# A LoRA transformer block in fp32: values made between the base products, and probabilities turned in fp32

## The reference, cut to what matters

```
x (8 batches, 128 tokens, 512)                      all in fp32
x = x + x @ W0[id0[b]].T                            base product, one 512x512 matrix per batch
q, k, v = lora(x; wq, aq, bq), lora(.. k), lora(.. v)   32 query heads, 8 key/value heads, D = 128
    lora(x; w, a, b) = x @ w + (x @ a[id1]) @ b[id1]    rank 16
q, k = rope(q), rope(k)                             out = q * cos + swapped(q) * sin
p = softmax(causal(q @ k.T / sqrt(D)));  o = p @ v
x = x + lora(o; wo, ao, bo)
x = x + LoRA 2 (A, B[id0]);  x = x + linear W3, b3 + LoRA 3[id2]
```

## Time and profile before

| what | us |
|---|---|
| median of 3 runs (839.33 to 841.19) | 840.07 |
| the profiled execution | 838.21 |
| its span, first to last instruction | 836.4 |
| PE busy in the span | 758.6 (91%) |
| DVE busy | 606.9 (73%) |
| ACT busy | 360.9 (43%) |
| POOL busy | 327.9 (39%) |
| mean granted TensorE clock | 0.958 of 2.4 GHz |

### The profile page before, as it was taken

One profiled execution on the slowest core, in us unless ns is written; L12 is line 12 of the kernel. 1 busy time (PEld: TensorE's weight loads), 2 busy tenths in 40 slices (PEclk: granted clock), 3 DMA queues, 4 the chain that ended last, 5 costly groups with the idle time before them and its releaser, 6 DMA issues. The chain is left out here.

```text
span 836.4 us, 13875 instructions
## 1 busy us (share of the span) xinstructions
PE 758.6 (91%) x4356; PEld 629.8 (75%) x4356; DVE 606.9 (73%) x1502; ACT 360.9 (43%) x967; POOL 327.9 (39%) x277
## 2 busy tenths in 40 slices
PE   3768849899689999999999999999999999987798
PEld 2657638687568888888888888888888888875586
DVE  3544266688488788789779778878877977854883
ACT  3545142311164464446446355446444644542550
POOL 3412620154274355337336426435524633510320
PEclk8878969999799999999999999999999999999799
DMA  8772977876205024122303303402412110610502
GB/s 296 274 225 72 281 235 190 230 244 189 65 7 170 1 64 139 39 63 67 108 17 108 113 0 97 141 0 63 138 38 63 63 38 27 136 17 4 127 17 85
DMA packets 61802, 88.92 MB, mean 106 GB/s; under 512 B 18550, under 2 KB 36118, under 8 KB 58054
## 3 DMA queue, kind: packets, MB, share of 16 engines
q1 hardware_dynamic: 59442, 81.92, 32.6%
q0 software_dynamic: 2176, 6.49, 2.6%
q10 hardware_dynamic: 148, 0.07, 0.0%
HBM read 73.50 MB, written 20.73 MB: 113 GB/s over the span
## 5 line engine op out<-in xcount | busy, mean ns | idle before, releaser
L944 POOL TENSOR_TENSOR prob<-prob,rinv 128x512 f32<-128x512 f32 x64 | 66.6, 1040 | 199.2 <-DVE rinv L1034 199.2
L889 ACT ACTIVATE prob<-sm,nmax 128x128 f32<-128x128 f32 x256 | 99.8, 391 | 80.3 <-DVE nmax L1015 80.3
L937 POOL TENSOR_TENSOR qt<-qc,qs 128x512 f32<-128x512 f32 x60 | 96.7, 1611 | 96.1 <-DVE qs L973 96.1
L1111 PE MATMUL ps_out<-wo_hi,ot_hi 128*128 128x512 f32 x256 | 106.4, 416 | 5.9 <-DVE ot_lo L992 3.7
L80 PE MATMUL ps_q<-x1t_hi,blk_hi 128*128 128x512 f32 x240 | 100.7, 420 | 0.0
L1113 PE MATMUL ps_out<-wo_hi,ot_lo 128*128 128x512 f32 x256 | 100.7, 393 | 0.0
L1112 PE MATMUL ps_out<-wo_lo,ot_hi 128*128 128x512 f32 x256 | 99.7, 390 | 0.0
L1015 DVE CUSTOM_DVE_ANT_0 sm<-ps_s,maskbias 128x128 f32<-128x128 f32 x256 | 58.7, 284 | 54.2 <-issue 54.1
L81 PE MATMUL ps_q<-x1t_lo,blk_hi 128*128 128x512 f32 x240 | 95.8, 399 | 0.0
L82 PE MATMUL ps_q<-x1t_hi,blk_lo 128*128 128x512 f32 x240 | 95.7, 399 | 0.0
L973 DVE TENSOR_TENSOR qs<-ps_q,sin_t 64x512 f32<-64x512 f32 x120 | 82.6, 688 | 3.7
(11 more groups left out here) (194 smaller groups left out, 1871.4 us busy)
## 6 DMA issues: line engine op xcount, KB each, us to landing
wo_raw<-in_wo SPq DMA_DIRECT2D x8, 1024.0 KB, 4.9
raw_w<-in_wq SPq DMA_DIRECT2D x8, 1024.0 KB, 5.3
w_raw<-in_w SPq DMA_DIRECT2D x7, 1024.0 KB, 9.7
raw_b<-bq_sel SPq DMA_DIRECT2D x56, 128.0 KB, 4.7
raw_b<-bkv_sel SPq DMA_DIRECT2D x16, 256.0 KB, 6.6
v_hi_d<-v_hi SPq DMA_DIRECT2D x16, 256.0 KB, 3.1
v_lo_d<-v_lo SPq DMA_DIRECT2D x16, 256.0 KB, 3.8
k_rot<-kr SPq DMA_DIRECT2D x16, 256.0 KB, 2.9
```

What stands on the lines that cost most here:

```text
L889: e = act.activation(prob[i][:, h, :], sm[:, h, :], ACT.Exp, bias=nmax[i][:, h:h + 1], scale=-1.0, accum_out=rsum[i][:, h:h + 1])
L937: pool.tensor_tensor(qt[:, half, h, :], qc[:, :], qs[:, :], ALU.add).then_inc(q_done, 1)
L944: pool.tensor_tensor(prob[i][:, :, :], prob[i][:, :, :], rinv[i][:, :].unsqueeze(2).broadcast_to([P, G, T]), ALU.mult).then_inc(prob_done, 1)
L1111: pe.matmul(ps_out[:, :], ot_hi[:, q], wo_hi[:, h, :], start=(h == 0), stop=False)
```

## The change

The base block and the projection block become one block of 38 steps (s = 0 to 37). In step s PE does, where they exist: value or key unit n = s - 2, base product s, adapters s - 1, and the turning of sum s. Block tiles get new names (`wgt_hi`, `wgt_lo`, `packs` for `blk_hi`, `blk_lo`, `blk_b`), and a table, `PIECES`, says in which step each piece of a weight block or LoRA pack is split. To make room, raw tiles lie over tiles of later blocks (`w0_raw` in `qt` and the trigonometry tables, for instance).

The diff, cut to its core:

```diff
-    bkv_sel = nc.dram_tensor("bkv_sel", (B, R, 2, KVH * D), F32, kind="Internal").ap()
...
+        PIECES = {1: [(0, "w", k) for k in range(KC)] + [(0, "b", 0)], 2: [(0, "b", 1)], 3: [(0, "b", 2), (0, "b", 3)],
+                  4: [(1, "b", 0), (1, "b", 1)], 5: [(1, "b", 2), (1, "b", 3)],
+                  7: [(1, "w", 0), (1, "w", 1)], 8: [(1, "w", 2), (1, "w", 3)],
+                  10: [(2, "b", 0)], 11: [(2, "w", 0)], 12: [(2, "w", 1)], 13: [(2, "w", 2)], 14: [(2, "w", 3)],
+                  15: [(2, "b", 1)], 16: [(2, "b", 2)], 17: [(2, "b", 3)]}
+        for k in range(KC):
+            PIECES[18 + k] = [(3, "w", k)]
+            PIECES[22 + k] = [(3, "b", k)]
...
+        def load_block_b(dma, j):
+            src = (bv, bv, bk, bk)[j]
+            cols = slice(j % 2 * GW, (j % 2 + 1) * GW)
+            for b in range(B):
+                pick = dma.value_load(id_rows[0:1, 1, b:b + 1], min_val=0, max_val=src.shape[0] - 1)
+                for quad in range(4):
+                    at = 32 * quad + R * (b % 2)
+                    dma.dma_start(raw_b[at:at + R, b // 2, :], src[bass.DynSlice(pick, 1), :, cols].rearrange("a r n -> (a r) n")).then_inc(raw_b_in, 16)
...
+                    load_w0(0)
+                    load_w0(1)
+                    sp.wait_ge(ids_in, 32)
+                    load_x(0)
+                    load_a(0)
+                    load_block_w(sp, 0)
+                    load_block_b(sp, 0)
+                    load_x(1)
+                    load_a(1)
+                    load_w0(2)
+                    load_x(2)
+                    load_a(2)
+                    for b in range(RAW, B):
+                        load_w0(b)
+                        load_x(b)
+                        load_a(b)
                         if b == 5:
...
+                            sp.wait_ge(w_lo_done, KC)
+                            load_block_w(sp, 1)
+                        if b == 6:
+                            sp.wait_ge(b_lo_done, PAIRS)
+                            load_block_b(sp, 1)
+                    sp.wait_ge(b_lo_done, 2 * PAIRS)
+                    load_block_b(sp, 2)
...
+                    sp.wait_ge(b_lo_done, 3 * PAIRS)
+                    load_block_b(sp, 3)
+                    for m in range(VU):
+                        g, h = divmod(m, 2)
+                        sp.wait_ge(k_done, m + 1)
+                        sp.dma_start(k_rot[g, :, h * HT:(h + 1) * HT], kr[h]).then_inc(k_out[h], 16)
...
+                                act.wait_ge(raw_b_in, RAW_B_IN[j])
+                                if j >= 2:
+                                    act.wait_ge(p_ready, UNITS * (j - 1))
+                                act.activation(packs[PACK[j]][:, k, :], raw_b[:, k, :], ACT.Copy).then_inc(b_hi_done, 1)
...
+                        if s >= 2:
+                            split_pieces(s)
...
+                        if 1 <= n <= VU:
+                            store_v(n - 1)
...
+                        if 8 <= s < 8 + B:
+                            gather_bq(s - 8)
...
+                        if 19 <= s < 19 + B:
+                            gather_last(s - 19)
+                        if n >= VU:
+                            m = n - VU
+                            pool.wait_ge(k_mult, 3 * m + 3)
+                            if 2 <= m < VU:
+                                pool.wait_ge(k_out[m % 2], 16 * (m // 2))
+                            rotated = kr[m % 2] if m < VU else qt[:, 0, m - VU, :]
+                            pool.tensor_tensor(rotated, k_cos[m % 2], k_sin[m % 2], ALU.add).then_inc(k_done, 1)
...
-                            act.activation(p_hi[:, :, :], prob[i][:, :, :], ACT.Copy).then_inc(p_hi_done, 1)
-                            dve.tensor_scalar(rsum_low[:, :], rsum[i][:, :], 1.0 / P_SCALE, None, ALU.mult).then_inc(sum_done, 1)
-                            dve.tensor_tensor(p_lo[:, :, :], prob[i][:, :, :], p_hi[:, :, :], ALU.subtract).then_inc(p_lo_done, 1)
...
                         for h in range(G):
-                            pe.matmul(ps_t[:, h * T:(h + 1) * T], p_hi[:, h, :], ident_h[:, :], start=True, stop=False)
-                            mm = pe.matmul(ps_t[:, h * T:(h + 1) * T], p_lo[:, h, :], ident_h[:, :], start=False, stop=True)
+                            mm = pe.transpose(ps_t[:, h * T:(h + 1) * T], prob[t_parity][:, h, :], ident[:, :])
...
                             scores(t, g, b)
+                            if not first or b >= 1:
+                                turn(t - 1, (b - 1) % B)
                             if b < HALF:
                                 queries(t, 1, b, None if first else (G * g, PAIRS * g))
...
-                            if not first or b >= 1:
-                                turn(t - 1, (b - 1) % B)
```

More of the change, by code:

```diff
@@ new lines, in program @@
+        a_hi = [sb(early, f"a_hi{i}", [P, KC, 3, R], F32R) for i in range(2)]
+        a_lo = [sb(early, f"a_lo{i}", [P, KC, 3, R], F32R) for i in range(2)]
+        axn = [sb(early, f"axn{i}", [P, 3, 4, 2, R], F32R) for i in range(2)]
+        early.close()
+        wo_raw = sb(attn, "wo_raw", [P, G, HID])
+        ao_raw = sb(attn, "ao_raw", [P, B, G, R])
+        ao_flat = ao_raw[:, :, :, :].rearrange("p b h r -> p b (h r)")
+        kt = sb(attn, "kt", [P, NT])
+        v_hi3 = sb(attn, "v_hi3", [P, B, D], F32R)
@@ L145, in load_block_b @@
[L145 to L149, removed]
+        wq_in = sem(attn, "wq_in")
+        wo_in = sem(attn, "wo_in")
+        bq_in = [sem(attn, f"bq_in{i}") for i in range(2)]
+        ao_in = sem(attn, "ao_in")
+        kt_in = [sem(attn, f"kt_in{i}") for i in range(2)]
+        v_in = [sem(attn, f"v_in{i}") for i in range(2)]
@@ new lines, in program, with load_wq, load_bq @@
+        RAW_B_IN = (512, 1024, 1536, 2048, 2048 + 64)
+        def load_wq(dma, g):
+            dma.dma_start(raw_w[:, :, :], wq[bass.DynSlice(g, 1)].rearrange("a p c n -> p (a c) n")).then_inc(wq_in, 16)
+        def load_bq(dma, g, h):
+            for quad in range(4):
+                dma.dma_start(raw_b[32 * quad:32 * quad + 32, 2 * h:2 * h + 2, :],
+                              bq_sel.rearrange("(c two) r n -> (two r) c n", two=2)[:, 2 * h:2 * h + 2, bass.DynSlice(g * GW, GW)]
+                              ).then_inc(bq_in[h], 16)
@@ L705, in _ @@
+                    for s in range(LAST):
+                        n = s - 2
                         if 4 <= n < VU + 4:
@@ L731, in program @@
+                        if s < B:
+                            product(s)
+                        if 1 <= s <= B:
+                            adapters(s - 1)
+                        if s < B:
+                            turn_x1(s)
         with ExitStack() as c:
-            wq_raw, bq_raw, wq_hi, wq_lo, bq_pack = raw_w, raw_b, blk_hi[0], blk_lo[0], blk_b[0]
+            wq_raw, bq_raw, wq_hi, wq_lo, bq_pack = raw_w, raw_b, wgt_hi[0], wgt_lo[0], packs[0]
             wo_hi = sb(c, "wo_hi", [P, G, HID], F32R)
@@ L891, in slots @@
                             e.then_inc(exp_done, 1)
-                            if not first or b >= 1:
-                                pt(t - 1, None if not first else t - 1)
                             if b < HALF and not last:
@@ L963, in _, with rotate @@
                 def _(dve):
[L964 removed]
+                    def rotate(n, half, i):
                         tok = slice(half * HT, (half + 1) * HT)
@@ L1022, in slots @@
                                 add(t - 3, (b - 3) % B)
+                            if not first or b >= 1:
+                                pt(t - 1)
                             if b == 2:
```

883 lines of the change are left out of this document (409 added, 474 removed).

## The result

| | before | after |
|---|---|---|
| median of 4 runs | 839.82 us (839.33 to 841.19) | 850.25 us (848.79 to 851.92) |
| ratio | | 1.0122, 95% interval 1.0098 to 1.0146 |
| profiled execution, its span | 838.21, 836.4 | 849.50, 847.8 |
| first scores | 225.8 | 236.9 |
| attention, first scores to last output | 545.3 | 546.5 |

The change made the kernel 1.2% slower. The forecast was 834.0, range 816 to 849, mostly on the faster side. 850.25 lies outside the range and on the other side.

The account below looks back on a forecast made before the run. TensorE was taken to bound attention; transfers, splits and waits the first 156 us. Span 836.4 + 5.8 (later attention start) - 11.5 (attention) = 830.7, profiled execution 832.5, median 834; range 816 to 849.

Parts of the forecast that it names:

- 4.5 + 2.5 - 0.8 = 6.2; I take -6.0: Attention slots 3 to 59: faster turns save 4.5, longer slots vanishing save 2.5, later query additions cost 0.8; -6.0 us.
- 0.8 for all: Attention: 0.05 us for each of 15 places where scores may wait for the queries GpSimd adds last.
- rival C: Attention, b = 3 and 7: rotation too late in each half, 15 x 0.5 = 7.5 us, 841.5; chance 0.11.
- the 0.36 longer slot: Attention, slots before b = 4: turned low part waits behind the query rotation; removing this saves 7 x 0.36 = 2.5 us.
- 3.4 + 2.2 = 5.6: Ends of attention: first three slots and slots 60 to 62 save 3.4 us, the last probabilities' dropped steps 2.2.
- the loss for the second block: Merged block, step 4: ACT waits for the second block of packs on SP's queue, TensorE loses 17 us.
- the 4.5 us for stored values: Value units from step 10: waits for stored values to land, an eighth of 35.3 us, range 0 to 18.
- rival A: Merged block: 16-row issues take half, or additions catch up in the keys; about -11 us, 823; chance 0.24.
- 75 forecast: Keys and queries: 60.6 us at pace plus 14 for the fourth block of packs and GpSimd's gathers.
- priced that for step 4 (2 us): Merged block, step 4: some 2 us lost to TensorE's lowered clock, on top of the 17 us wait.
- B: Merged block, steps 8 to 17: value stores issued by ACT block it and TensorE; +11 us, 845; chance 0.20.
- D: Attention: fp32 turns lower TensorE's granted clock, 64 x 0.42 = +27 us, 861; chance 0.03.

Follow-up runs that it names:

- the run with both edits on the kernel before: Kernel before with the change's attention, outputs in head order 0, 2, 3, 1, and `pt_lo` behind the rotation in slots b = 7: 831.5 us (0.9909).
- the fastest kernel: Changed kernel: head order 0, 2, 3, 1; `pt_lo` late in b = 7; packs later; fourth spread; adapter numbers kept; batch 1, matrix 2 loads first: 812.87 us (0.9682).

## Why the prediction was wrong, step by step

The forecast is 16 us too low. In the profiled executions the steps miss by: attention 12.7, the keys 5.4 by their end, the last block -1.

**The failing step: "4.5 + 2.5 - 0.8 = 6.2; I take -6.0" for slots 3 to 59.** Measured +6.4. Of it, against 8.43 a slot:

- Slots b = 2: +7.0. It was not in the sum and in no rival. I had named what `pt_lo` stands ahead of on VectorE in b = 3 and 7 (the rotation), but not in b = 2, where the next instruction is the piece of `wo_lo` that TensorE needs in that slot. That VectorE's work "lies beside TensorE" was read from the average slot. The run with attention alone has the same loss there, +7.0, and the run with the head order changed has -0.3 in its place, so this wait is the loss. Why the piece is late is shown less well. By the traces `pt_lo` puts it 0.60 us back and the longer first piece 0.50, and slot 58, with `pt_lo` in place and a quick first piece, loses 0.46 instead of 1.15. So the order of instructions that I had overlooked is about half of it; why the `wo_lo` pieces became longer, and what `pt_lo` alone costs, no run tried.
- Slots b = 7: +1.45, b = 0, 3 and 4 together +1.05, where I had 0.8 for all. In b = 7 this is rival C at half its price, and the run with `pt_lo` late in b = 7 shows the cause. The others are 0.1 longer than 8.39. Behind b = 3 the scores start 0.05 after the end of GpSimd's addition (336.64, 336.59) and 0.32 instead of 0.23 after the matmul before them, which looks like C as well; in b = 0 and 4 the second score starts 0.21 behind the first and not 0.11. In the run with both edits on the kernel before, b = 0 is back at 8.40 and b = 3 and 4 stay at 8.49 and 8.50; what makes these two longer was not tried.
- b = 3: the 0.36 longer slot is gone. There were six of them and not the seven that I had counted, so -2.2 of the 2.5 forecast.
- A turn: slots without any wait are 8.39, so they gain 0.04 and not 0.08. From the first of the four turns (319.53) to the next matmul it is 0.35, where the eight fp16 matmuls took 0.43 (406.49 to 406.92); but the scores ahead of the turns take 0.89 and not 0.81, so that the first output matmul stands 4.36 into the slot in both kernels. The gain lies behind it: the outputs take 2.80 from their first matmul to the first of `ps_ao` (run with both attention edits), and 2.85 with the old turns right ahead of them (run with the merged block alone). That is 0.05, where my sum had counted on 0.08.

The ends of attention: -1.8 for slots 0 to 2 and -3.3 for the last four; forecast 3.4 + 2.2 = 5.6 for both, measured 5.1. Right.

**The merged block up to the keys: right in the main, in part by luck.** A block of 32 DMAs was to take 20 us (19.3), TensorE to start again at 41.5 (41.4, though with the turn of sum 1 and not with base product 2), step 4 near 60 (60.0), the loss for the second block to be 17 us (16.8), the keys to start at 149 (148.1). The views that gave this were SP's queue and the order of instructions, not a busy share. The last number is right by luck: the eight value units from step 10 on took 24.3 us without one wait, so that the 4.5 us for stored values did not arise there, and in their place step 10 came 2 us late and the keys waited 1.8 for the third pack. What this stretch also shows is that my rival A (an issue of 16 rows takes half) is false, at 0.47 to 0.52 for each DMA.

**The keys and queries: 75 forecast, 82.1 measured.** The holes were sized well in sum: beyond the normal pace they are 3.5, 5.1, 1.0, 1.2 and 3.1, together 13.9 (forecast 14), though not where I put them. The fourth block is issued 7.8 us into the keys and not at their start, since it waits for the pieces of the third. GpSimd's pace with the gathers is not 3.9 but 2.7 (180.66 to 183.34 above), which is below the 3.03 of a unit, so the gathers did not set the pace. The holes end with a pack (three) or with VectorE's key products (two), and these two stand behind GpSimd's wait of 6.8 us for one key store. What was missing is the clock. The granted clock is 0.90 over the 82 us, and it is lower behind the three longer holes (columns as in the windows above, the granted clock stands third from the end):

```profile
155.00:160.00 5.00, 5.00 (x17) 4.02 (x16) 4.17 (x7) 1.68 (x3) 1.91 (x2) 0.66 0.67 179
184.00:187.00 3.00, 3.00 (x9) 2.32 (x8) 2.91 (x5) 0.00 (x0) 2.58 (x4) 0.53 0.55 151
215.00:220.00 5.00, 5.00 (x12) 3.94 (x13) 4.85 (x8) 0.00 (x0) 2.80 (x3) 0.50 0.59 213
```

Behind the two short ones, of 1.0 and 1.2 us, it stays at 1.00. TensorE is busy for 68.5 us with 60.6 us of work at full clock. I had priced that for step 4 (2 us) and put it at nothing here, 7.6 to 7.9 us. In the fastest kernel the same units, with fewer holes, are busy for 65.1 us at a clock of 0.93.

**Rivals.** B: none of ACT's 32 issues of value stores took more than 1.3 us, where B had 8; what ACT waits for is landing, 16.3 us in six waits, the longest 6.4. The value units did not feel these, but a piece of the third pack stands on ACT behind the last of them (3.9 us, to 152.54), and the hole of 3.5 us in the keys ends with that piece. So stores on ACT did cost something, 3.5 us at most there, by landing and not by issue; B decided from 8 us on, and did not come about. D: the granted clock over attention is 1.00, with 256 fp32 turns in it. The rule of the Trainium skill ("TensorE: Matmul & The Clock Gate", Part 4) that transposes don't count as busy like matmuls had no effect that these runs show, with some 0.4 us of turns in 8.4.

**The chances.** Slower had 0.29. The side was lost by the wait for `wo_lo`, which no rival named, and the range by two terms (`wo_lo`, clock) with the same sign: without either of them the time would have been within it.

## What to carry to other kernels

An instruction that moves ahead on an in-order engine has to be followed slot by slot, with the list of what it now stands ahead of in each of them; one slot in eight with a due piece, and a second with a tight one, were enough here to turn a gain of 7 to 8 us into nothing. When something is late at its consumer, the consumer's own order is the cheaper place to mend: moving the producer displaced the next due instruction, while taking the late head last brought 7.2 us in the slots and cost 1.7 once. A group of small DMAs is a stretch of its queue (32 of them 19 us), and it belongs where nothing behind it, on the queue or on the engine that waits for it at the head of its list, is due.

## What the runs showed of the hardware that I had not expected

- After the holes of 3.1, 3.5 and 5.1 us in the keys TensorE ran on at a granted clock of 0.50 to 0.66; after those of 1.0 and 1.2 us it stayed at 1.00. In all, 13.9 us of holes came with 7.6 to 7.9 us lost in slow matmuls.
- VectorE's subtraction for `wo_lo` took 1.44 to 1.66 us in slot 10, where GpSimd made subtractions of its own at the same time, and 0.69 for the first piece of slot 58, where GpSimd began its own only at 732.05; the same operation on a weight piece took 0.69 in the keys while GpSimd stood still (192.14). That GpSimd's work is the cause was not tried. In the kernel before, the second piece shows 0.79, and the tiny step behind it 1.19 instead of 0.17; TensorE starts head 1 at 314.25, before that step ends at 314.58. With pieces that grow by 0.5 us and more, counting the 0.6 us of `pt_lo` alone would not have given the loss.
- Reading a number from memory into a register on SP held its queue for some 0.4 to 0.5 us net, a fifth of the 2.4 us that a reading and four DMAs take together.
